# VectorE takes over the difference of state and candidate, GpSimd the low half of the stepped state

## The reference

```python
A = (adj != 0).astype(x.dtype)
h = x
for l in range(weight.shape[0]):          # 5 layers
    m = jnp.einsum('bnd,de->bne', h, weight[l])
    agg = jnp.einsum('bij,bid->bjd', A, m)
    h = _gru_cell(agg, h, w_ih, w_hh, b_ih, b_hh)
...
def _gru_cell(m, h, w_ih, w_hh, b_ih, b_hh):
    gi = m @ w_ih.T + b_ih
    gh = h @ w_hh.T + b_hh
    i_r, i_z, i_n = jnp.split(gi, 3, axis=-1)
    h_r, h_z, h_n = jnp.split(gh, 3, axis=-1)
    r = jax.nn.sigmoid(i_r + h_r)
    z = jax.nn.sigmoid(i_z + h_z)
    n = jnp.tanh(i_n + r * h_n)
    return (1.0 - z) * n + z * h
...
x = _layernorm(x + _L0_gnn_ref(...), axis=-1)
x = _layernorm(x + _L1_gnn_ref(...), axis=-1)
```

## Time and profile before

| | before |
|---|---|
| median of 3 runs | 534.87 us (534.04 to 535.93) |
| profiled execution, as a whole | 537.68 us |
| its span, first to last instruction | 534.5 us |
| TensorE busy | 518.4 us, 97% |
| VectorE busy | 436.2 us, 82% |
| ScalarE busy | 368.5 us, 69% |
| GpSimd busy | 249.3 us, 47% |
| mean granted TensorE clock | 0.989 |

### The profile page before, as it was taken

How to read it: one execution, slowest core, us unless ns; L and a number is a source line. 1 busy time by engine, 2 the same in 40 slices (tenths; PEclk the granted TensorE clock), 3 DMA queues, 4 the chain that set the end, 5 groups by cost and what they waited for, 6 DMA issues and landing times.

```text
span 534.5 us, 8522 instructions
## 1 busy us (share of the span) xinstructions
PE 518.4 (97%) x2991; PEld 443.5 (83%) x2991; DVE 436.2 (82%) x970; ACT 368.5 (69%) x680; POOL 249.3 (47%) x299
## 2 busy tenths in 40 slices
PE   7999999999999999999999999999999999999991
PEld 6888889888888888888888889888888888888871
DVE  4479755899979886789979986778988998787887
ACT  2447665667775767688786676687786678786745
POOL 6658513348542343457642255445543235432334
PEclk9999999999999999999999999999999999999995
DMA  5768610000000010000000000000000000010002
GB/s 136 182 169 223 154 41 11 1 1 0 2 0 1 1 33 21 21 20 21 1 1 1 1 0 21 21 20 21 0 2 0 2 1 20 21 41 0 1 0 79
DMA packets 35578, 17.28 MB, mean 32 GB/s; under 512 B 4321, under 2 KB 35498, under 8 KB 35538
## 3 DMA queue, kind: packets, MB, share of 16 engines
q1 hardware_dynamic: 32233, 14.99, 10.6%
q10 hardware_dynamic: 2665, 1.54, 1.0%
q0 software_dynamic: 640, 0.22, 0.3%
HBM read 12.54 MB, written 4.19 MB: 31 GB/s over the span
## 4 chain that ended last, share of the span: by engine, by line
PE 93%; DVE 3%; ACT 1%; DMA 1%; POOL 1%; ACTq 1%; issue 0%; DVEq 0%
PE p L1251 20%; PE p L1253 20%; PE p L1252 20%; PE p L1245 13%; PE p L1238 8%; PE p L1131 3%; PE p L1105 2%; PE p L1124 1%; PE p L1114 1%; PE p L1049 1%; DMA zg<-in_L_gnn_weight_dram 1%; PE p L1169 1%; PE p L1055 1%; ACTq L267 0%; PE p L1161 0%; DVE st L919 0%
## 5 line engine op out<-in xcount | busy, mean ns | idle before, releaser
L485 POOL TENSOR_TENSOR dg<-hT,ng 128x512 f32<-128x512 f32 x80 | 126.4, 1580 | 256.0 <-ACT ng L701 256.0
L1251 PE MATMUL p<-ghi,wf 128*128 128x512 f32 x240 | 101.1, 421 | 0.0
L1251 PE MATMUL p<-hhi,wh 128*128 128x512 f32 x237 | 99.7, 421 | 0.0
L1253 PE MATMUL p<-ghi,wf 128*128 128x512 f32 x240 | 94.4, 393 | 0.0
L1252 PE MATMUL p<-glo,wf 128*128 128x512 f32 x240 | 93.7, 390 | 0.0
L1253 PE MATMUL p<-hhi,wh 128*128 128x512 f32 x237 | 93.2, 393 | 0.0
L1252 PE MATMUL p<-hlo,wh 128*128 128x512 f32 x237 | 92.4, 390 | 0.0
L1004 DVE SCALAR_TENSOR_TENSOR cg<-p,biasc,rg 128x512 f32<-128x512 f32 x80 | 59.8, 748 | 38.2 <-ACT rg L683 37.1
L683 ACT ACTIVATE rg<-p,gb 128x512 f32<-128x512 f32 x80 | 55.4, 692 | 34.9 <-PE p L1253 29.0
L701 ACT ACTIVATE ng<-cg,biasc 128x512 f32<-128x512 f32 x80 | 57.8, 723 | 23.1 <-DVE cg L1007 22.9
L1245 PEld LDWEIGHTS p<-an,nat 128*128 128x128 f32 x512 | 66.9, 191 | 5.1
(11 more groups left out here) (155 smaller groups left out, 848.8 us busy)
## 6 DMA issues: line engine op xcount, KB each, us to landing
xn<-in_x_dram SPq DMA_DIRECT2D x8, 512.0 KB, 4.9
an<-in_adj_dram SPq DMA_DIRECT2D x8, 512.0 KB, 7.6
out_dram<-xn SPq DMA_DIRECT2D x15, 256.0 KB, 2.3
xt<-in_x_dram SPq DMA_DIRECT2D x16, 50.0 KB
w<-in_L_gnn_W_dram ACTq DMA_DIRECT2D x1, 640.0 KB, 5.6
w<-in_L_gnn_W_dram SPq DMA_DIRECT2D x1, 640.0 KB, 5.9
zg<-in_L_gnn_weight_dram ACTq DMA_DIRECT2D x1, 320.0 KB, 4.1
xt<-in_x_dram SPq DMA_DIRECT2D x8, 36.0 KB
```

What stands on the lines that cost most here:

```text
L485: nc.gpsimd.tensor_tensor(dg[:, w.k % 2, :], hT[:, w.slot, :], ng[:, w.k % 2, :], ALU.subtract).then_inc(d_ok, 1)
L1251: MM(bank[:], w[:, 0, cols], xhi, start=start, stop=False)
L1253: return MM(bank[:], w[:, 1, cols], xhi, start=False, stop=stop)
```

## The change

Two operations change places. The difference `hT - ng` leaves GpSimd and becomes the first instruction of VectorE's `end_step`. The low half of a stepped state, `hT - hhi`, leaves VectorE and stands in GpSimd's list where the difference was. The low halves of states that enter, 16 in all, stay on VectorE. TensorE waits for a new semaphore, `low_ok`, where its window's state has been stepped, and for `lo_ok` where it has entered.

```diff
+def stepped(m):
+
+    return m // PER * (PER - SLOTS) + m % PER - SLOTS + 1
...
@@ gpsimd, each window
-                pool.wait_ge(n_ok, w.k + 1)
-                nc.gpsimd.tensor_tensor(dg[:, w.k % 2, :], hT[:, w.slot, :], ng[:, w.k % 2, :], ALU.subtract).then_inc(d_ok, 1)
+                if w.k and ALL_WINDOWS[w.k - 1].turn == "step":
+                    o = (w.k + 2) % SLOTS
+                    pool.wait_ge(hi_ok, made(w.k + 2))
+                    nc.gpsimd.tensor_tensor(hlo[:, o, :], hT[:, o, :], hhi[:, o, :], ALU.subtract).then_inc(low_ok, 1)
@@ vector, end_step
                 p = (k - 1) % 2
+                dve.wait_ge(n_ok, k)
+                TT(dg[:, p, :], hT[:, s, :], ng[:, p, :], ALU.subtract).then_inc(d_ok, 1)
                 dve.wait_ge(d_ok, k)
                 TT(dg[:, p, :], zg[:, p, :], dg[:, p, :], ALU.mult).then_inc(e_ok, 1)
@@ vector, each window
-                if k and ALL_WINDOWS[k - 1].turn == "step":
-                    lo_state(k + 2)
@@ tensor, each window
-                    pe.wait_ge(lo_ok, made(k))
+                    if w.l:
+                        pe.wait_ge(low_ok, stepped(k))
+                    else:
+                        pe.wait_ge(lo_ok, w.sg * SLOTS + w.slot + 1)
```

More of the change, by code:

```diff
@@ L246, in build @@
         r_ps, i_ps, z_ps, T_ps, X_ps, F_ps, G_ps = map(sem, ("r_ps", "i_ps", "z_ps", "T_ps", "X_ps", "F_ps", "G_ps"))
-        r_ok, z_ok, n_ok, t1_ok, c_ok, d_ok, e_ok, h_ok = map(sem, ("r_ok", "z_ok", "n_ok", "t1_ok", "c_ok", "d_ok", "e_ok", "h_ok"))
+        r_ok, z_ok, n_ok, t1_ok, c_ok, d_ok, e_ok, h_ok, low_ok = map(sem, (
+            "r_ok", "z_ok", "n_ok", "t1_ok", "c_ok", "d_ok", "e_ok", "h_ok", "low_ok"))
         hi_ok, lo_ok, nat_ok, ghi_ok, glo_ok = map(sem, ("hi_ok", "lo_ok", "nat_ok", "ghi_ok", "glo_ok"))
@@ L639, in state @@
                 if visit < SLOTS:
-                    act.wait_ge(lo_ok, made(visit))
+                    act.wait_ge(lo_ok, visit + 1)
                 else:
```

## The result

| | before | changed |
|---|---|---|
| median of 5 runs each, same chip | 534.87 us (534.04 to 535.93) | 556.95 us (555.58 to 558.17) |
| ratio | | 1.0407, interval 1.0388 to 1.0426 |
| span of the profiled execution | 534.5 us | 555.2 us |
| TensorE, VectorE, ScalarE, GpSimd busy | 518.4, 436.2, 368.5, 249.3 us | 526.6, 439.1, 369.2, 210.3 us |

A forecast was written before the change was run, and what follows sets the result against it. TensorE, busy 466.84 of 467.00 us, was taken as the bound; the lengthened VectorE loop would make turns wait, 11.3 + 4.3 + 2.7 = 18.3 us on the 534.87 median, giving 553.2 us, range 547 to 559.

The forecast's parts named there:

- the margin: In a plain window, TensorE's turn has 0.45 us in hand behind the new hT before it must wait.
- The step: Difference between VectorE's second cg and the product into dg lengthens the path to hT by 0.71 us, at least 0.61.
- The turns without margin: Six turns that already wait for hT, with no shortened queue in front, pay 0.71 us each: 4.3 us.
- 42 with a margin: Turns following hT by 0.34 to 0.57 us wait 0.71 less their margin, on average 0.27 each: 11.3 us.
- 24 turns pay nothing: Turns behind graph-convolution work come 0.9 us or more after hT, so they lose nothing.
- The low half off VectorE: 64 of 80 hlo move to GpSimd: helps only where VectorE's queue delays cg; on GpSimd it costs zero.
- Contention: Nine hlo held by GpSimd's difference get 1.1 us each back on VectorE; holds of the new trio counted as nothing.
- the eight: Turns following hT by 0.05 to 0.20 us, seven with VectorE's queue late, lose 0.1 to 0.6 each: 2.7 us.
- The rival from the Trainium skill: GpSimd's masks in windows 11 and 13 hold VectorE's difference, product and sum: +4.5, 557.7 us; chance 0.08.
- The margin did not hide the step: Rival: plain windows absorb the difference, only six turns without margin pay: +4.3, 539.2 us; chance 0.05.
- VectorE's shorter queue: Rival: without 64 hlo and nine holds, seven turns start up to 0.28 us earlier: 2.0 us, 532.9; chance 0.02.
- The clock did not fall: Rival: idling between turns lowers TensorE's clock, 0.8 us in each of 56 waiting windows: 45, about 598 us; chance 0.03.

The follow-up runs named there:

- Run 3: Changed kernel with VectorE's difference moved ahead of the first cg, where VectorE waits for the sigmoid: 539.62 us, 1.0081 of the kernel before.
- run 9: Changed kernel with GpSimd waiting for VectorE's sum ahead of each mask and the spreading, and in window 2 ahead of the low half: 552.98 us, 1.0307.
- run 1: Kernel before with only the difference moved to VectorE's end of a step, the low half staying on VectorE: 560.78 us, ratio 1.0467.
- run 8: Changed kernel with VectorE's difference right behind glo, a window earlier, and on GpSimd in windows 0, 1, 77, 78 and 79: 540.07 us, 1.0080.
- run 2: Changed kernel with the difference back on GpSimd behind the low half, so only the low half moved: 545.72 us, 1.0176 of the kernel before.

## Why the prediction was right

The mechanism came as forecast, and 553.2 us against 556.95 is 3.8 us too low. The two can be told apart.

**What bounds it, and the margin: right.** The margin of 0.45 us was read from two turns, and the runs with half, one and two differences put it there: 0.45 of step is just hidden, 0.72 loses 0.28, 1.44 loses 1.00.

**The step: right.** I took 0.71 for a step that turned out as 0.72 (0.61 in front of the difference, 0.72 behind it). Run 3 shows that the loss is one of place: the same instruction on VectorE outside the loop costs a fifth, and part of that is the clock.

**The classes of turns: right, but for window 2.** The 56 turns that wait are those of the sum. The turns without margin lose 0.72 to 0.77; of the 42 with a margin 37 lose 0.25 to 0.33, windows 52 and 63 0.14 and 0.21, window 11 of three rounds 0.70 to 0.74. "24 turns pay nothing" was wrong for one: I had looked at the turn's distance behind `hT` alone, and `hT` has a second reader, ScalarE's `hhi`, with the graph convolution's work behind it in the list. With the holds off it still lost 0.35 (run 9), half of the step.

**The low half off VectorE: right.** Nobody waits for it on GpSimd. `hlo` of entering states is at 0.69 us now, as here at the end of such a window, where the earlier trace rows had 1.77:

```profile
304.95 0.69 DVE L898 TENSOR_TENSOR hlo<-hT,hhi 128x512 fp32r<-128x512 f32 x1
```

**Contention: the term that was sized wrong.** I gave GpSimd's holds nothing, on the word of one product that ran at full speed in the middle of a mask. That product began 1.5 us into the mask. The trace before had the other case as well, in window 12 of the third round:

```profile
371.65 1.94 POOL L420 TENSOR_SCALAR an<-an 128x512 f32<-128x512 f32 x1
...
371.93 0.88 DVE L902 TENSOR_TENSOR dg<-zg,dg 128x512 f32<-128x512 f32 x1
```

A product that begins 0.28 us into the mask takes 0.88. One that begins with it is held longer (window 11 of the changed kernel), and so is a difference beside the low half (window 2), which I had not priced at all. Run 9 takes both away: from first to last turn 17.67 of 20.44 us stay, and with its last step's 0.65 that makes 18.3, my sum. From the first turn to the last one of all the changed kernel lost 21.2, so my sum lacked 2.9 us, and 2.9 go with the holds and what they set off. In the span it is 2.4, since the profiled execution came to its first turn 0.5 earlier. That the sum is met to a tenth is partly luck: in run 9 the 42 turns with a margin lose 0.5 us more than forecast, the 24 another 0.5, and the eight 1.1 less; and by its ratio run 9 loses 16.4 us (15.2 to 17.7). Of the 3.8 us by which the forecast missed the median, some 0.9 us stay open.

The rival from the Trainium skill, "SBUF — State Buffer", section "Who interferes with whom", was therefore half right. For GpSimd's large instructions with two SBUF inputs the traces agree with its rule that a VectorE instruction with two SBUF inputs is locked out for the whole of them (the product of 4.31 us). For the mask, which has one input, they differ: the hold ends 0.6 us into its 1.93, and the product at 124.91 was free. The measurement decides. My rival priced the masks of windows 11 and 13 at 0.3 us in one and 1.2 in the other; window 13 shows no hold, and window 11 one of 0.46. Its 557.7 us is nearer to the measured time than my forecast, by luck: 1.2 of the 2.9 us came from window 2, which it didn't name.

**The other rivals.** The margin did not hide the step. VectorE's shorter queue gave 3 to 5 us, seen only beside run 1. The clock did not fall in the changed kernel's stalls, as it did once in run 3: it was granted at 1.00 from 50 to 538 us, with TensorE busy for 477.27 of 488.00:

```profile
50.00:538.00 488.00, 477.27 (x2690) 397.66 (x2690) 392.92 (x807) 337.80 (x613) 171.62 (x208) 1.00 0.06 15
```

## What to carry to other kernels

Before an operation changes engines, ask whether its new place lies inside the loop that ends in the bottleneck's next wait, and measure that loop's margin: from the end of the producer to the consumer, less the same distance where the consumer did wait. VectorE was less busy by share after the change and the kernel slower; with the difference in the loop it cost 22 us, with it outside, on the same engine, 4. And when work goes to GpSimd, look at what VectorE runs at that moment, not at whether GpSimd has time: a wait that keeps the two apart took 4 to 6 us off, though one put in the wrong window made a norm late and cost 1.1 us in each of three rounds.

## What the runs showed of the hardware

- GpSimd's low half and difference (128x512, two float32 inputs), and each part of its spreading, hold a VectorE instruction with two SBUF inputs that begins after them until they end; a held one of 128x512 ends 0.54 to 0.55 us after that (302.81 against 302.27 in the trace before), the one of nine columns 0.01 (123.33 against 123.32 in run 8, 1.25 us instead of 0.16). GpSimd's instructions with two tiny inputs don't: VectorE's low half at 116.53 in the trace before took 0.66 us within one of 128x9 that went from 115.91 to 117.73.
- Where two GpSimd instructions stand back to back, a VectorE instruction that is held by the first mostly gets in between: 58 times of 67 in the thirteen traces, and then GpSimd's second one takes longer (the mask 2.37 us instead of 1.93, the low half 1.74 instead of 1.28). Nine times it was held on, which gave 4.31 us for a product and 3.25 for a difference of 0.69. No run shows what decides.
- The mask, GpSimd's `tensor_scalar` of 128x512 with one input, 1.93 us, holds for its first 0.6 us only. In the traces 32 instructions of VectorE's that began before or in that time ended 1.15 us behind the mask's start, such as those at 57.51 (mask from 56.36) and 122.62 (121.46) in the changed kernel, 134.65 (133.50) in run 2 and 54.95 (53.80) in run 3. One doesn't fit: in run 1 a product that began 1.18 us into a mask, at 56.66, took 1.04 us; a second mask followed there.
- A dependent instruction of VectorE's starts 0.72 us behind one of 0.69 (some 0.73), an independent one 0.60 to 0.63, where nobody holds them.
- In run 3 TensorE was busy for 4.53 of 6.70 us, and then its granted clock was 0.50 from 61.7 to 65.1 us; its products took 0.63 us instead of 0.39 or 0.40. Neither the 56 short waits of the changed kernel nor one of 2.99 us in the profiled execution of run 2 (TensorE busy for 0.44 of the 3.40 us up to 135.40) brought it down.
